# Two-layer graph transformer on one Trainium2 core: last residual steps by row block, graph probabilities scaled on ScalarE, and the final midpoints' scalars in one chain

## The reference

```python
xn = _layernorm(x)
x = x + _L1_gnn_ref(xn, ...) + _L1_mix_ref(xn[None], ...)[0]
x = x + _L1_ffn_ref(_layernorm(x)[None], ...)[0]

# in _L1_gnn_ref, for 4 heads of 64
alpha = p / (denom[dst] + 1e-16)           # p = exp(e - m[dst]), denom its sum
out = jax.ops.segment_sum(alpha[..., None] * xl[src], dst, num_segments=n)
return out.reshape(n, HID) @ W_up          # 256 -> 1024

# in _L1_ffn_ref: top 2 of 16 experts, then the shared one
def _lresnet(x, y, w):
    z = x + w * y
    inner = -z[..., :1] ** 2 + jnp.sum(z[..., 1:] ** 2, -1, keepdims=True)
    return jnp.sqrt(C) * z / jnp.sqrt(jnp.clip(-inner, EPS))
y = y0; y = _lresnet(y, out_of_expert, weight)   # twice per row
z = _lmlp(xt, Ws1, bs1, Ws3, bs3, Ws2, bs2)
out = _lresnet(y, z, 1.0)
```

## Time and profile before

| | us |
|---|---|
| median of 3 runs | 1875.64 |
| profiled execution, its own time | 1872.85 |
| its span | 1871.0 |
| TensorE busy in the span | 1781.3 |
| VectorE busy | 739.1 |
| ScalarE busy | 390.9 |
| granted TensorE clock, mean | 0.978 of full |

### The profile page before, as it was taken

One profiled execution on the slowest core, in us unless ns is written; L12 is line 12 of the kernel. 1 busy time (PEld: TensorE's weight loads), 2 busy tenths in 40 slices (PEclk: granted clock), 3 DMA queues, 4 the chain that ended last, 5 costly groups with the idle time before them and its releaser, 6 DMA issues. The chain is left out here.

```text
span 1871.0 us, 22026 instructions
## 1 busy us (share of the span) xinstructions
PE 1781.3 (95%) x8526; PEld 1129.8 (60%) x8526; DVE 739.1 (40%) x1518; ACT 390.9 (21%) x719; POOL 636.8 (34%) x538
## 2 busy tenths in 40 slices
PE   9999999989999999998999999999999999999953
PEld 5475446445545777546777765677654776776731
DVE  6884113224425231453455556430621222223226
ACT  1000000001411011002677754121000322222222
POOL 0657872220000286777888510000300322222210
PEclk9999999998999999999899999999999999999986
DMA  9663124370710153333222154160411899999952
GB/s 350 183 187 74 2 46 113 82 227 5 303 47 4 48 159 96 91 95 87 56 56 57 27 140 119 46 246 4 136 62 45 311 414 401 406 419 396 412 151 79
DMA packets 104069, 289.09 MB, mean 155 GB/s; under 512 B 61941, under 2 KB 65239, under 8 KB 91836
## 3 DMA queue, kind: packets, MB, share of 16 engines
q1 hardware_dynamic: 28634, 224.83, 32.4%
q0 software_dynamic: 68160, 51.85, 12.4%
q10 hardware_dynamic: 7198, 11.36, 2.0%
HBM read 257.19 MB, written 30.32 MB: 154 GB/s over the span
## 5 line engine op out<-in xcount | busy, mean ns | idle before, releaser
L381 PE MATMUL bank<-wring,turned_a 128*125 128x512 f32 x480 | 207.6, 593 | 1.6 <-DVE turned_a L752 0.7
L606 POOL DMA_INDIRECT table_d<-wring x85 | 172.4, 2028 | 102.0 <-issue 55.2
L967 POOL DMA_INDIRECT wring<-xl_d,wring x85 | 105.9, 1245 | 259.4 <-DMA xr_d<-flat_b 233.5
L381 PEld LDWEIGHTS bank<-wring,turned_a 128*125 128x125 f32 x480 | 89.6, 188 | 115.3 <-issue 114.2
L2235 PEld LDWEIGHTS bank<-picked_t,wring 128*128 128x128 f32 x1280 | 143.7, 192 | 7.6 <-issue 7.3
L2235 PE MATMUL bank<-picked_t,wring 128*128 128x128 f32 x1280 | 145.6, 276 | 0.1
L397 PE MATMUL bank<-flat_d,wring 128*128 128x312 f32 (+1 forms) x512 | 135.0, 426 | 0.0
L980 POOL DMA_INDIRECT score_d<-wring x85 | 111.0, 1306 | 69.3 <-DMA score_d<-wring 46.6
L397 PEld LDWEIGHTS bank<-flat_d,wring 128*128 128x128 f32 x512 | 96.7, 189 | 37.9
L967 POOL DMA_INDIRECT wring<-xr_d,wring x85 | 109.2, 1285 | 25.9 <-issue 23.8
L2250 PE MATMUL bank<-wring,unit_t 128*128 128x512 f32 x160 | 74.0, 605 | 0.0
(11 more groups left out here) (438 smaller groups left out, 2745.7 us busy)
## 6 DMA issues: line engine op xcount, KB each, us to landing
wring<-in_experts SPq DMA_DIRECT2D x60, 2048.0 KB, 11.3
wring<-in_L_Ws SPq DMA_DIRECT2D x6, 2048.0 KB, 28.1
table_d<-eq_buf SPq DMA_DIRECT2D x2, 3072.0 KB, 29.0
score_d<-no_edge SPq DMA_DIRECT2D x2, 3072.0 KB, 33.0
wring<-table_d POOLq DMA_DIRECT2D x10, 610.4 KB, 7.3
wring<-score_d SPq DMA_DIRECT2D x5, 1093.8 KB
...
```

The source lines that it names most:

```text
L381: ins = pe.matmul(bank[0:R, :], act_t[:, k, tok(t)], w[:, k * HALF:(k + 1) * HALF], start=(k == 0), stop=(k == chunks - 1))
L606: pool.indirect_dma_start(out=tables_d[b % 2], out_offset=bass.IndirectOffsetOnAxis(ap=edge_at[:, b:b + 1], axis=0), in_=edge_sums[:, b, : ...
L967: pool.indirect_dma_start(out=to[:, g % 2, j, :], out_offset=None, in_=table, in_offset=bass.IndirectOffsetOnAxis(ap=index[:, b:b + 1], ax ...
```

## The change

Four parts.

1. **Graph probabilities.** ScalarE multiplies the probabilities of each head by 1/sum (`scale_probs`, four operations of 125x625 per row block), VectorE no longer builds the diagonals, and TensorE turns the scaled probabilities by transposes. The first turn moves from tile 2 to tile 3.
2. **W_up by row block.** `up_product(t)` for t = 0 to 3 goes between the Wo tiles, the last one behind them. VectorE adds it (`add_up`), takes the statistics and the variance of that block, ScalarE its root (`act_tile_root`), and VectorE normalises blocks 0 to 3 at the end of the mixing Block, block 4 in the next. `shared` gets a place of its own, that was `turned_a`, so that it can be written in that Block.
3. **Start of the expert Block.** No `pe_keep_busy`; TensorE transposes row block by row block, and the logits of block t wait for its copies alone, and for the gate's weights alone. The three biases count on `bias_in`, for which ScalarE and VectorE wait later.
4. **Tail.** The two rows of a token lie side by side in DRAM (8 KB runs). VectorE takes three dot products per row block as they land. All four roots are in one chain, which also scales the factors by the last inverse. TensorE puts `res` into PSUM ahead and adds the scaled sum of the routed rows to it; VectorE adds inverse * `shared` block by block in the same pass. For the last block GpSimd adds `res` and ScalarE's product.

Two further edits: the fill of `score_d` uses rows of 384 instead of 512 numbers (1.5 KB instead of 2 KB runs), and some semaphores are merged.

```diff
-gat_t = q1_t[:, 6:8, :]
+gat_t = sq
+shared = region_a[0:R, :].rearrange("r (t d) -> r t d", d=D)
...
-TURN_AT = {2: 0, 4: 1, 6: 2, 7: 3, 8: 4}
+TURN_AT = {3: 0, 4: 1, 6: 2, 7: 3, 8: 4}
...
-tops_made, exps_made, diags_made = sem("tops_made"), sem("exps_made"), sem("diags_made")
+UP_AT = {6: 0, 7: 1, 8: 2, 9: 3}
...
+def add_up(v, t):
+    after(v, dve_step)
+    for h in range(2):
+        cols = slice(h * HALF, (h + 1) * HALF)
+        v.tensor_tensor(res[:, t, cols], dring.consume(v)[0:R, :], res[:, t, cols], ALU.add).then_inc(d_emptied, 1)
+        v.wait_ge(d_emptied, dring.taken)
+        dve_half_stats(v, res, t, h)
+    ln_tile[t] = dve_tile_var(v, t, 1e-5)
...
         def turn_probs(t):
...
-            pe.wait_ge(diags_made, t + 1)
+            pe.wait_ge(probs_scaled, t + 1)
...
-                    ins = pe.matmul(bank[0:R, tok(h)], probs[:, t % 2, h, tok(a)], scale_diag[t % 2][:, h, :],
-                                    start=True, stop=True)
+                    ins = pe.transpose(bank[0:R, tok(h)], probs[:, t % 2, h, tok(a)], ident[0:R, 0:R])
                 ins.then_inc(s_filled, 1)
...
             ins.then_inc(s_filled, 1)
+            gat_marks["rows", t] = sring.made
...
+        up = []
...
+        def up_product(t):
+            if t == 0:
+                up.append(wt.take(pe))
+            pe.wait_ge(s_emptied, gat_marks["rows", t])
+            for h in range(2):
+                bank = dring.produce(pe)
+                for k in range(2):
+                    ins = pe.matmul(bank[0:R, :], gat_t[:, k, tok(t)],
+                                    up[0][:, k * D + h * HALF:k * D + (h + 1) * HALF],
+                                    start=(k == 0), stop=(k == 1))
+                ins.then_inc(d_filled, 1)
...
+            if n in UP_AT:
+                up_product(UP_AT[n])
...
-        sring.wait_empty(pe)
-        pe_gemm_slot(pe, gat_t, 2)
+        up_product(T - 1)
+        wt.free(dring.filled, dring.made)
...
-            soft.mark(v.reciprocal(gden[:, t, :], gden[:, t, :]))
-            after(v, soft)
-            if t >= 2:
-                v.wait_ge(s_filled, gat_marks["turned", t - 2])
-            v.tensor_tensor(scale_diag[t % 2], ident[0:R, 0:R].unsqueeze(1).to_broadcast([R, GH, R]),
-                            gden[:, t, :].unsqueeze(2).to_broadcast([R, GH, R]), ALU.mult).then_inc(diags_made, 1)
+            v.reciprocal(gden[:, t, :], gden[:, t, :]).then_inc(dens_made, 1)
...
-        after(v, dve_step)
-        dve_add_to_res(v)
+            if n in UP_AT:
+                add_up(v, UP_AT[n])
+        for t in range(T - 1):
+            dve_tile_norm(v, res, shared, t, ln_tile[t])
...
+        def scale_probs(t):
+            s.wait_ge(dens_made, t + 1)
+            for h in range(GH):
+                ins = s.activation(probs[:, t % 2, h, :], probs[:, t % 2, h, :], ACT.Copy, scale=gden[:, t, h:h + 1])
+            ins.then_inc(probs_scaled, 1)
...
         exps(1)
+        scale_probs(0)
...
             if t:
                 keep_rows(t - 1)
+            if t + 1 < T:
+                scale_probs(t + 1)
             if t + 2 < T:
                 exps(t + 2)
+            if t >= 3:
+                act_tile_root(s, t - 3)
         keep_rows(T - 1)
+        act_tile_root(s, 2)
+        act_tile_root(s, 3)
...
     def _(pe):
-        pe_keep_busy(pe, 26)
-        pe.wait_ge(normed.sem, normed.n + T)
-        pe_transposes(pe, shared)
-        pe_wait_evacuated(pe)
-        pe.wait_ge(ffn_in, 64)
-        pe_logits(pe, x3_t, gate16, NE1)
+        turned = [pe_turn(pe, shared, t, normed.n - (T - 1) + t + 1) for t in range(T)]
+        pe.wait_ge(ffn_in, 16)
+        pe_logits(pe, x3_t, gate16, NE1, before=lambda t: pe_wait_turned(pe, turned[t]))
...
-        dve_layer_norm(v, res, shared, 1e-5, halves_done=True)
-        evac_transposes(v, dring, 0, x3_t, lambda o, i, k: v.tensor_copy(o, i))
...
+        add_up(v, T - 1)
+        keep_turned_rows(v, dring, 0, x3_t, 0, copy)
+        dve_tile_norm(v, res, shared, T - 1, ln_tile[T - 1])
+        for t in range(1, T):
+            keep_turned_rows(v, dring, 0, x3_t, t, copy)
...
-        sp.dma_start(bs13[:, 0, :], a["L1_bs1"]).then_inc(ffn_in, 16)
-        sp.dma_start(bs13[:, 1, :], a["L1_bs3"]).then_inc(ffn_in, 16)
-        sp.dma_start(bs2_b[:], a["L1_bs2"].to_broadcast([R, D])).then_inc(ffn_in, 16)
+        sp.dma_start(bs13[:, 0, :], a["L1_bs1"]).then_inc(bias_in, 16)
+        sp.dma_start(bs13[:, 1, :], a["L1_bs3"]).then_inc(bias_in, 16)
+        sp.dma_start(bs2_b[:], a["L1_bs2"].to_broadcast([R, D])).then_inc(bias_in, 16)
...
-picks = wring[:].rearrange("p s c -> p (s c)")[0:R, 0:2 * T * D].rearrange("r (n t d) -> r n t d", n=2, t=T)
+picks = wring[:].rearrange("p s c -> p (s c)")[0:R, 0:2 * T * D].rearrange("r (t n d) -> r n t d", n=2, t=T)
...
+        halves = [slice(h * HALF, (h + 1) * HALF) for h in range(2)]
+        pe.wait_ge(to_root.sem, 2)
+        for t in range(T - 1):
+            for h, cols in enumerate(halves):
+                pe.matmul(banks[2 * t + h][0:R, :], ident[0:R, 0:R], res[:, t, cols], start=True, stop=False)
         for t in range(T - 1):
             pe.wait_ge(second_added, t + 1)
-            for h in range(2):
-                cols = slice(h * HALF, (h + 1) * HALF)
-                pe.matmul(banks[2 * t + h][0:R, :], ident[0:R, 0:R], picks[:, 0, t, cols],
-                          start=True, stop=False)
-                ins = pe.matmul(banks[2 * t + h][0:R, :], ident[0:R, 0:R], shared[:, t, cols],
+            for h, cols in enumerate(halves):
+                ins = pe.matmul(banks[2 * t + h][0:R, :], ident[0:R, 0:R], picks[:, 0, t, cols],
                                 start=False, stop=True)
             ins.then_inc(z_made, 1)
...
-            tail.mark(v.tensor_tensor_reduce(products[:], picks[:, 0, t, :], picks[:, 1, t, :], 1.0, 0.0,
-                                             ALU.mult, ALU.add, small[:, DOT.start, t:t + 1]))
-            after(v, tail)
+            for n, (left, right) in enumerate(((picks[:, 0, t, :], picks[:, 1, t, :]),
+                                               (picks[:, 0, t, :], shared[:, t, :]),
+                                               (picks[:, 1, t, :], shared[:, t, :]))):
+                tail.mark(v.tensor_tensor_reduce(products[:], left, right, 1.0, 0.0, ALU.mult, ALU.add,
+                                                 small[:, DOT.start + n, t:t + 1]))
+                after(v, tail)
...
         tiny(small[:, C.start, :], small[:, A, :], inv, ALU.mult)
-        v.sem_inc(scales_made, 1)
         tiny(small[:, C.start + 1, :], w[:, 1, :], inv, ALU.mult)
         tiny(y0, y0, small[:, WT.start + 1, :], ALU.add)
         tiny(y0, y0, inv, ALU.mult)
-        for t in range(T):
-            v.wait_ge(first_scaled, t + 1)
-            step(v.scalar_tensor_tensor(out=picks[:, 0, t, :], in0=picks[:, 1, t, :],
-                                        scalar=small[:, C.start + 1, t:t + 1], in1=picks[:, 0, t, :],
-                                        op0=ALU.mult, op1=ALU.add))
-            tail.mark(v.tensor_tensor_reduce(products[:, 1:], picks[:, 0, t, 1:], shared[:, t, 1:], 1.0, 0.0,
-                                             ALU.mult, ALU.add, small[:, DOT.start + 1, t:t + 1]))
-            step(v.tensor_copy(picks[:, 0, t, 0:1], y0[:, t:t + 1]))
-            v.sem_inc(second_added, 1)
-        tail.mark(v.tensor_tensor(picks[:, 1, T - 1, :], picks[:, 0, T - 1, :], shared[:, T - 1, :], ALU.add))
+        tiny(small[:, TMP.start + 1:TMP.stop, :], small[:, C, :], small[:, DOT.start + 1:DOT.stop, :], ALU.mult)
         tiny(tmp[0], y0, t3, ALU.mult)
-        tiny(tmp[0], tmp[0], small[:, DOT.start + 1, :], ALU.subtract)
+        tiny(tmp[0], tmp[0], tmp[1], ALU.subtract)
+        tiny(tmp[0], tmp[0], tmp[2], ALU.subtract)
         step(v.tensor_scalar(tmp[0], tmp[0], 2.0, 2.0, ALU.mult, ALU.add))
         inverse_norm(tmp[0])
-        for t in range(T - 1):
+        tiny(small[:, C, :], small[:, C, :], inv.unsqueeze(1).to_broadcast([R, 2, T]), ALU.mult)
+        tiny(shared[:, :, 0], y0, t3, ALU.add)
+        v.sem_inc(scales_made, 1)
+        def add_second(t):
+            v.wait_ge(first_scaled, t + 1)
+            v.scalar_tensor_tensor(out=picks[:, 0, t, :], in0=picks[:, 1, t, :],
+                                   scalar=small[:, C.start + 1, t:t + 1], in1=picks[:, 0, t, :],
+                                   op0=ALU.mult, op1=ALU.add).then_inc(second_added, 1)
+        def add_shared(t):
             v.wait_ge(z_made, t + 1)
             for h in range(2):
                 cols = slice(h * HALF, (h + 1) * HALF)
-                ins = v.scalar_tensor_tensor(out=res[:, t, cols], in0=banks[2 * t + h][0:R, :],
-                                             scalar=inv[:, t:t + 1], in1=res[:, t, cols],
+                ins = v.scalar_tensor_tensor(out=res[:, t, cols], in0=shared[:, t, cols],
```

(33 more changed lines are left out.)

59 lines of the change are left out of this document (33 added, 26 removed).

## The result

| | before | after |
| --- | --- | --- |
| median, us | 1875.35 (1873.63 to 1876.47, 4 runs) | 1854.80 (1848.41 to 1856.28, 4 runs) |
| profiled execution: own time, span, us | 1872.85, 1871.0 | 1855.41, 1853.6 |
| TensorE, VectorE, ScalarE, GpSimd busy, us | 1781.3, 739.1, 390.9, 636.8 | 1773.3, 743.3, 404.6, 644.7 |

The ratio is 0.9876 (95%: 0.9854 to 0.9898). The forecast was 1854.0 us.

What follows compares the result with a forecast made beforehand. TensorE, busy 1781.3 of 1871.0 us, was taken as the bound, with the tail a chain beside which nothing runs. Terms -11.4 - 2.6 - 7.6 = -21.6 took 1875.64 to 1854.0 us; range 1848.5 to 1862.

Steps and rivals of the forecast that it cites:

- Turns, waits and W_up, -11.4: Graph attention: transposes for matmuls -11.3 us, waits of 1.07 and 0.48 gone, 1.5 of new waiting: -11.4 us.
- The walk through ScalarE's queue: Between tiles 3 and 4, turn 1's fifth bank waits for ScalarE's first copy: 1.5 us (bounds 0.5 and 6.1).
- The joint, -4.1 + 1.5 = -2.6: End of W_up to end of logits: 22.0 us becomes 17.9, less 1.5 lost to the half clock: -2.6 us.
- 1.7 us lost, part of it under VectorE's 5.0: +1.5: Joint: 3.0 us idle halves TensorE's clock for 3.4 us of work; cost +1.5 us, bounds 0 and 5.
- Rival A: Joint: clock stays down until within the logits, 5 us lost in place of 1.5, 1857.5 us; chance 0.12.
- Landing and start of the chain, 0: Tail: routed blocks land about 3.8 us apart, VectorE's three dot products end it; chain starts unchanged (bounds -0.8, +1.2).
- I take the nearer, 283: Tail reads: 8 KB runs reach 283 GB/s instead of 263; +1.2 us if the landing stays.
- Chain +3.15: Tail: seven more small operations 1.4 us, fourth root and inverse 1.35, two for the factors 0.4: +3.15 us.
- Pass -9.5: Tail: VectorE's two passes over the rows, 23.5 us, become one of 13.9: -9.5 us.
- GpSimd's sum ...: nothing: Tail, last block: GpSimd's sum takes about 2 us, twelve microseconds ahead of its use, and costs nothing.
- Output -1.2: End of tail: last bytes come about 4.8 us after VectorE instead of 6.0: -1.2 us.
- rival C: Tail gives 3 to 4 us less: half-clock identity matmuls (+3) or 8 KB runs bring nothing (+1.2); 1857.5 us; chance 0.11.

Runs made afterwards that it cites:

- diag: Changed kernel with the turns again as matmuls with VectorE's diagonals and without ScalarE's scaling: 1859.97 us.
- more_exps: Changed kernel with two more exponentials of 500 numbers on ScalarE before each of the exponentials of row blocks 2 to 4: 1851.33 us.
- the second pair: Second profiled traces of the unedited kernels before and after the change, each run again; medians 1871.48 us (before) and 1844.55 us (after).
- rows4k: Changed kernel with the two routed rows of a token apart again, read in runs of 4 KB instead of 8 KB: 1850.67 us.
- last_on_dve: Changed kernel with VectorE itself adding the last block's shared part; ScalarE's scaling of `shared` and GpSimd's sum gone: 1847.65 us.
- the second series: Unaltered kernels before and after the change, timed again: 1844.55 us against 1874.15, ratio 0.9844.

## Why the prediction was right, point by point

- **Turns, waits and W_up, -11.4.** Wo to W_up's end was 122.2 us and is 110.4: -11.8. The turns gave 5 x 2.18 = 10.9 of the 11.3, at 2.35 each and not 2.26. The walk through ScalarE's queue found the right turn, tile and cause; its wait was 0.75, not 1.5, since copies behind one another take 0.49 and not 0.59 each. diag confirms the transposes (10.6 for all), more_exps the queue.
- **The joint, -4.1 + 1.5 = -2.6.** 22.0 us became 17.0 with the clock kept, 17.4 with it lost: -5.0 for the -4.1, the 0.9 from an idle time of 2.6 for 3.0 and from 5.5 for 5.9 between it and the logits. The step that failed is "1.7 us lost, part of it under VectorE's 5.0: +1.5". Nearly all of it lay under VectorE: 0.4. The sum itself had VectorE as the bound there, and transposes at half speed ran over it by 0.5 only; the prediction did not carry that through. Rival A is out: the clock was back before the logits. Against the rule of the Trainium skill (TensorE: Matmul & The Clock Gate, Part 4) that the full clock does not engage for transposes, diag has rows in which TensorE ran nothing but transposes, from its idle time to 1219.5:

```profile
1216.00:1218.00 2.00, 2.00 (x11) 2.00 (x10) 1.89 (x6) 1.03 (x3) 0.39 (x1) 0.50 0.92 371
1218.00:1219.50 1.50, 1.50 (x15) 1.50 (x14) 1.50 (x4) 0.83 (x2) 0.00 (x0) 0.92 0.48 155
```

- **Landing and start of the chain, 0.** Mis-sized: 30.83 us behind the last `small_out` became 32.24, +1.4 (31.19 became 32.60 in the second pair, +1.4 too). The blocks still land 4.1 apart, and three products follow the last. The step that failed is "I take the nearer, 283"; the bound named beside it, +1.2, was the case. By the Trainium skill's rule on 512 B and more (DMA: Bandwidth & Descriptors, Specifications), 4 and 8 KB are alike, which is the case of that bound. Before against after agrees with it (last block at 28.0 and 28.4, then 28.2 and 28.7), rows4k against after does not.
- **Chain +3.15.** 6.78 became 9.93: exact, by counting instructions at 0.2 and taking the fourth root from a row.
- **Pass -9.5.** 23.5 us became 14.7: -8.7. Missing is the second addition at 2.55 for 1.28. The sentence "GpSimd's sum ...: nothing" failed: nobody waits for it, but it slows the engine beside it. GpSimd's sum ends at 1835.29 + 2.36 = 1837.65, the addition 1.08 us later, at 1838.73 (1.08 in the second trace too), as if most of it stood still meanwhile. The Trainium skill (Trainium Architecture — The Big Picture, What this means for kernel authors) calls the port pair of VectorE and GpSimd an exclusive lock; these rows and last_on_dve agree, and the prediction should have used it.
- **Output -1.2.** 6.0 became 4.8: right. The tail in all: -5.5 and -6.0, forecast -7.6. It gave 1.6 to 2.1 us less, between the forecast and rival C, which held 3 to 4: the landing that C named came, its half clock did not (granted 0.96 to 1.00 under the pass), and GpSimd's sum it did not name.
- **Sum.** -11.8 - 4.5 - 5.5 = -21.8 against -21.6: turns and joint gave 2.3 us more than forecast and the tail 2.1 less. That these misses cancel is luck. Not in the sum are 2.7 us ahead of Wo, and 1.7 between logits and tail, where behind the same idle time of 1.20 us one trace loses the clock and the other does not. Both went against the change in this pair and make its spans differ by 17.4 only; the second series, with 29.6 us between its medians, had them at least in part the other way by this reading, which is not shown, as the kernel before has no trace from that series. Its 1844.55 would lie outside of the forecast range, which allowed 2 us for what differs between sessions; these traces need 12.
